# Attention inputs of a decoder: two-part f32r products, a second input buffer, and query and key parts stored once

## The reference, cut to what matters

```
# layer 0, context attention ("ci", then "ca"): queries from x, 1024 keys and values from the context
qh = split_heads(layernorm(x) @ wq.T + bq)
logits = einsum('bhqd,bhkd->bhqk', qh, kh) / sqrt(16)
x = x + (softmax(logits) @ vh) @ wo.T + bo
# layer 1, self-attention ("ai", then "aa"): queries, keys, values from n = layernorm(x), 512 keys
q, k, v = split(n @ qkv_w.T + qkv_b)
x = x + n + softmax(q @ k.T * 0.25) @ v @ fc_w.T + fc_b
```

## Time and profile before

| | us |
|---|---|
| time, median of 3 runs | 5387.59 (5381.12 to 5390.33) |
| profiled execution, its own time | 5385.85 |
| its span | 5384.0 |
| `ci`: first work to the start of `ca` | 913.63 to 984.21 |
| `ca`: first load issued, first scores | 984.21, 1039.29 |
| `ai`: first work to the start of `aa` | 2073.40 to 2193.98 |
| `aa`: first load issued, first scores | 2193.98, 2220.76 |
| mean granted clock of TensorE | 0.956 |

### The profile page before, as it was taken

The page is one execution under the profiler, slowest core; times in us unless marked ns, Lnnn a source line. Parts: engine busy times, 40 slices in busy tenths (PEclk is TensorE's granted clock), DMA queues, the critical chain, the costliest instruction groups (busy, mean ns, idle before and its releaser), DMA issues. The chain is left out here.

```text
span 5384.0 us, 70030 instructions
## 1 busy us (share of the span) xinstructions
PE 4890.0 (91%) x23500; PEld 2615.4 (49%) x23500; DVE 3692.4 (69%) x6760; ACT 2846.1 (53%) x6114; POOL 2464.0 (46%) x1429
## 2 busy tenths in 40 slices
PE   6899996699999798799879999999999999999955
PEld 5555554244444465344455555555555555555423
DVE  8666665588888575577646666666666666666588
ACT  5677772277777433466534444454444445444423
POOL 5555553200000111100037778777777777777700
PEclk9999998699999799799989999999999999999978
DMA  6577676533433004544363433343333333333100
GB/s 213 200 246 253 245 246 207 150 73 69 77 69 73 1 0 162 151 79 80 96 194 83 98 89 85 90 98 82 87 94 83 86 94 93 80 94 94 40 35 20
DMA packets 342964, 593.53 MB, mean 110 GB/s; under 512 B 38576, under 2 KB 131824, under 8 KB 341600
## 3 DMA queue, kind: packets, MB, share of 16 engines
q1 hardware_dynamic: 340448, 585.06, 40.4%
q10 hardware_dynamic: 2176, 4.19, 0.2%
HBM read 333.70 MB, written 221.25 MB: 103 GB/s over the span
## 5 line engine op out<-in xcount | busy, mean ns | idle before, releaser
L2539 POOL TENSOR_TENSOR la_acc<-la_acc,la_pr 128x1024 f32<-128x1024 f32 x704 | 1696.7, 2410 | 494.4 <-ACT la_pr L2497 459.0
L2497 ACT ACTIVATE la_pr<-la_s_ps 128x512 f32<-128x512 f32 x1536 | 793.9, 603 | 971.6 <-PE la_s_ps L2349 970.1
L2356 PE MATMUL la_o_ps<-la_pr,la_vf 128*64 128x512 f32 x3072 | 743.8, 605 | 0.0
L2348 PE MATMUL la_s_ps<-la_q_hl,la_k_hh 128*128 128x512 f32 x1536 | 691.8, 450 | 1.7 <-ACT la_q_hs L2473 1.4
L1757 DVE TENSOR_REDUCE ca_mx<-ca_m_ps 128x2 f32<-128x1024 f32 x512 | 600.7, 1217 | 132.9 <-PE ca_m_ps L1619 132.9
L1720 ACT ACTIVATE ca_pr<-ca_s_ps 128x512 f32<-128x512 f32 x1024 | 541.7, 600 | 255.8 <-PE ca_s_ps L1626 252.6
L2566 DVE TENSOR_REDUCE la_mx<-la_m_ps 128x2 f32<-128x1024 f32 x384 | 463.0, 1206 | 216.8 <-PE la_m_ps L2331 208.8
L2349 PE MATMUL la_s_ps<-la_q_hs,la_k_l 65*128 65x512 f32 x1536 | 608.0, 396 | 0.0
L2566 DVE TENSOR_REDUCE la_mx<-la_misc 128x2 f32<-128x1024 f32 x384 | 466.0, 1214 | 0.0
L113 POOL TENSOR_TENSOR ff_ln_var_eps<-ff_ln_mv,g_eps 128x4 f32<-128x4 f32 x32 | 6.7, 210 | 954.8 <-DVE ff_ln_mv L98 954.8
L2348 PEld LDWEIGHTS la_s_ps<-la_q_hl,la_k_hh 128*128 128x128 f32 x1536 | 290.0, 189 | 242.8 <-ACT la_pr L2497 103.9
(11 more groups left out here) (360 smaller groups left out, 8294.7 us busy)
## 6 DMA issues: line engine op xcount, KB each, us to landing
la_k_hh<-scratch_k_high SPq DMA_DIRECT2D x128, 512.0 KB, 6.5
scratch_k_high<-sc_k_high SPq DMA_DIRECT2D x128, 256.0 KB, 2.6
scratch_k_low<-sc_k_low SPq DMA_DIRECT2D x128, 256.0 KB, 2.8
la_w_parts<-scratch_w_parts SPq DMA_DIRECT2D x64, 512.0 KB, 6.2
la_k_l<-scratch_k_low SPq DMA_DIRECT2D x64, 512.0 KB, 8.4
la_vf<-scratch_xv SPq DMA_DIRECT2D x64, 512.0 KB, 4.1
ca_ks<-scratch_k_rows SPq DMA_DIRECT2D x128, 192.0 KB, 6.3
scratch_vaug<-sc_v SPq DMA_DIRECT2D x16, 1024.0 KB, 4.4
```

The lines of the kernel that those rows point to most:

```text
L2348: pe.matmul(s_ps[:, bank, :], k_hh[:, par, h, keys], q_hl[:, par, h, :], start=True, stop=False)
L2356: last = pe.matmul(o_ps[XD * h:XD * h + XD, :], vf[:, par, st, XD * h:XD * h + XD], pr[:, st % LAG, h, :], start=(st == 0), stop=(st == XT ...
L2497: act.activation(pr[:, st % LAG, h, :], s_ps[:, (2 * st + h) % 3, :], ACT.Exp, scale=scale).then_inc(p_done, 1)
L2539: pool.tensor_tensor(total, total, exps, ALU.add).then_inc(acc_done, 1)
```

## The change

It has four parts.

1. In `ai` the products run on two f32r parts of each operand: high x high, low x high and high x low in place of one f32 product. The weights are split once at the start (ACT copies, POOL subtracts), the turned input per batch (ACT copies `tp` to `x_hi`, DVE subtracts into `x_lo`). In `ci` the product stays f32.
2. The turned input has two buffers (`par`), PE turns batch b+1 ahead of the products of batch b, and normalising runs one batch further ahead. In `ci` POOL's memset of `v1` is gone.
3. `store_parts` writes each part once, four transfers of 256 KB for an operand and batch.
4. `load` repeats the high part: three query and three times `HALVES` key transfers of 16 partitions x 2 heads (64 KB each) stand where one and `HALVES` of 48 partitions stood. A load is 20 transfers in `ca` and 13 in `aa`. The bytes loaded are the same.

The old lines are in the functions above; of the removed ones only those of `store_parts`, the load and the shapes stand here.

```diff
-def store_parts(sp, stack, n, ready, parts, which, stored):
+def store_parts(sp, stack, n, ready, parts, stored):
     for part in range(PARTS):
-        slots = [s for s in range(SLOTS) if which[s] == part]
-        step = slots[1] - slots[0] if len(slots) > 1 else 1
         sp.wait_ge(*ready[part])
         for m in reversed(range(KD)):
-            rows = stack[n, 8 * m:8 * m + 8].rearrange("h (d s) t -> (h d) s t", s=SLOTS)
-            sp.dma_start(rows[:, slots[0]:slots[-1] + 1:step, :],
-                         parts[:, part, m, :].bitcast(F32).unsqueeze(1).broadcast_to([P, len(slots), T])).then_inc(stored, 16)
+            sp.dma_start(stack[n, part, P * m:P * (m + 1), :], parts[:, part, m, :].bitcast(F32)).then_inc(stored, 16)
...
+            w_hi = [pool_.sb(f"w_hi{i}", [P, KD, D], F32R) for i in range(len(names))]
+            w_lo = [pool_.sb(f"w_lo{i}", [P, KD, D], F32R) for i in range(len(names))]
+            x_hi = pool_.sb("x_hi", [P, 2, KD, T], F32R)
+            x_lo = pool_.sb("x_lo", [P, 2, KD, T], F32R)
+        else:
+            xT = pool_.sb("xT", [P, 2, KD, T])
...
+                    if b:
+                        pe.wait_ge(x_high, KD * b)
+                        if own_keys:
+                            pe.wait_ge(x_low, KD * b)
...
+                def project(b, i, ps, ready, low):
+                    par = b % 2
                     for m in range(KD):
+                        cols = slice(m * P, (m + 1) * P)
+                        if b:
+                            pe.wait_ge(low, KD * (b - 1) + m + 1)
+                        for c in range(KD):
+                            if own_keys:
+                                pe.matmul(ps[:, m, :], w_hi[i][:, c, cols], x_hi[:, par, c, :], start=(c == 0), stop=False)
+                                pe.matmul(ps[:, m, :], w_lo[i][:, c, cols], x_hi[:, par, c, :], start=False, stop=False)
+                                last = pe.matmul(ps[:, m, :], w_hi[i][:, c, cols], x_lo[:, par, c, :], start=False, stop=(c == KD - 1))
+                            else:
+                                last = pe.matmul(ps[:, m, :], w[i][:, c, cols], xT[:, par, c, :], start=(c == 0), stop=(c == KD - 1))
+                        last.then_inc(ready, 1)
...
+                turn(0)
+                for b in range(B):
+                    if b + 1 < B:
+                        turn(b + 1)
+                    pe.wait_ge(x_high, KD * (b + 1))
                     if own_keys:
+                        pe.wait_ge(x_low, KD * (b + 1))
+                        if b == 0:
+                            pe.wait_ge(w_low, Q + 1)
+                    elif b == 0:
+                        pe.wait_ge(w_loaded[Q], 16)
+                    project(b, Q, q_ps, q_ready, q_low)
                     if own_keys:
+                        if b == 0:
+                            pe.wait_ge(w_low, V + 1)
+                        project(b, K, k_ps, k_ready, k_low)
+                        values(b)
...
+                    for i in range(len(names)):
+                        act.wait_ge(w_loaded[i], 16)
+                        act.activation(w_hi[i][:, :, :], w[i][:, :, :], ACT.Copy).then_inc(w_high, 1)
...
+                def weight_low(i):
+                    pool.wait_ge(w_high, i + 1)
+                    pool.tensor_tensor(w_lo[i][:, :, :], w[i][:, :, :], w_hi[i][:, :, :].bitcast(F32), ALU.subtract).then_inc(w_low, 1)
+                norm.on_gpsimd(pool, 0, g)
+                if own_keys:
+                    weight_low(Q)
+                norm.on_gpsimd(pool, 1, g)
+                if own_keys:
+                    weight_low(K)
+                    weight_low(V)
+                    pool.memset(v1[:, :, :, :, :], 1.0).then_inc(ones_set, 1)
...
+                def low_x(b):
+                    par = b % 2
+                    for c in range(KD):
+                        dve.wait_ge(x_high, KD * b + c + 1)
+                        dve.tensor_tensor(x_lo[:, par, c, :], tp[:, c, :], x_hi[:, par, c, :].bitcast(F32),
+                                          ALU.subtract).then_inc(x_low, 1)
...
+                moments(0)
+                apply(0)
+                moments(1)
+                if own_keys:
+                    add_x(0)
+                    low_x(0)
+                apply(1)
+                moments(2)
+                for b in range(B):
+                    if own_keys and b + 1 < B:
+                        add_x(b + 1)
+                        low_x(b + 1)
+                    if b + 2 < B:
+                        apply(b + 2)
+                    low_parts(b, q_ps, bq, qparts, q_high, q_low)
+                    if b + 3 < B:
+                        moments(b + 3)
                     if own_keys:
+                        low_parts(b, k_ps, bk, kparts, k_high, k_low)
...
-                        rows = slice(64 * i, 64 * i + STACK)
                         heads = slice(u * GH + i, (u + 1) * GH, 2)
-                        sp.dma_start(qs[rows, u, :, :].bitcast(F32), io[qstack][b, heads].rearrange("h r t -> r h t")).then_inc(loaded[u], 16)
-                        for half in range(HALVES):
-                            sp.dma_start(ks[rows, u, :, half * T:(half + 1) * T].bitcast(F32),
-                                         io[kstack][b * HALVES + half, heads].rearrange("h r t -> r h t")).then_inc(loaded[u], 16)
+                        for s in range(SLOTS):
+                            rows = slice(64 * i + s * DH, 64 * i + (s + 1) * DH)
+                            src = io[qstack][b, QPART[s]].rearrange("(h d) t -> h d t", d=DH)[heads]
+                            sp.dma_start(qs[rows, u, :, :].bitcast(F32), src.rearrange("h d t -> d h t")).then_inc(loaded[u], 16)
+                            for half in range(HALVES):
+                                src = io[kstack][b * HALVES + half, KPART[s]].rearrange("(h d) t -> h d t", d=DH)[heads]
+                                sp.dma_start(ks[rows, u, :, half * T:(half + 1) * T].bitcast(F32),
+                                             src.rearrange("h d t -> d h t")).then_inc(loaded[u], 16)
...
-                        ("q_rows", (B, HEADS, STACK, T)), ("k0_rows", (2 * B, HEADS, STACK, T)), ("k1_rows", (B, HEADS, STACK, T))):
+                        ("q_rows", (B, PARTS, D, T)), ("k0_rows", (2 * B, PARTS, D, T)), ("k1_rows", (B, PARTS, D, T))):
```

169 lines of the change are left out of this document (74 added, 95 removed).

## The result

The changed kernel took 5363.47 us (median of six runs, 5360.86 to 5370.31) where the kernel before took 5383.82 us on the same chip (median of six, 5372.53 to 5390.33). The ratio is 0.9967, its 95% interval 0.9954 to 0.9981: 0.33% faster, beyond the 0.2% that can be told from no change. The forecast of 5383 was 20 us too high; the time lies inside the range of 5358 to 5425, near its lower end. It is rival A's 5362, but only a part of the reason is A's, as the trace shows. The profiled execution of the changed kernel has a span of 5359.4 us and a mean granted clock of 0.955.

A forecast was written before the change was run, and what follows sets the result against it. Bounds taken: TensorE in `ai`, a TensorE-ScalarE ring in `ci`, the DMA queue at the head of `ca`. Terms -22.7 - 7 + 14 + 9 + 2 = -4.7 us gave about 5383 us from 5387.59; range 5358 to 5425.

The forecast's parts named there:

- rival A: Loads of `ca` and `aa`: small loads are cheap, 0.45 to 0.5 us each by SP's issue; 5362 us, chance 0.33.
- its own signs: Prediction wrong if a 64 KB load's price is outside 0.55 to 0.66 us or `ai`'s head takes over 5 us longer.
- t: Price of one 64 KB load to 16 partitions in `ca` and `aa`: taken as 0.60 us, between 0.45 and 1.23.
- Products of two parts: `ai`: 9.8 us a batch instead of 13.19, copy wait gone, longer head; -22.7 us, between -25 and -17.
- D: Rival: DVE bounds `ai` at 10.8 us a batch through tp's PSUM buffer; +8 us, 5391 us, chance 0.05.
- Two buffers in `ci`: `ci`: TensorE's ring opens, DVE becomes the bound, 6.2 us a batch against 7.0; -7 us, bounds -10 and -3.
- Stores: Input phases and scan: smaller stores on a queue that isn't late in either phase; 0, in the scan -2 to +2.
- Loads: Three 64 KB loads for each 192 KB one: +14 us head of `ca`, +9 head of `aa`, +2 steady `aa`.
- C: Rival: loads become the bound of `aa`, from 0.64 us a load; given 5415 us, chance 0.25.
- The sign that was to tell A from B: Window inside `ca`'s first loads: near 107 GB/s shows the forecast, 150 GB/s shows cheap small loads.
- B: The forecast itself: a 64 KB load costs about 0.57 to 0.66 us; 5383 us, range 5374 to 5398, chance 0.37.
- Sum: Whole kernel: -22.7 - 7 + 14 + 9 + 2 = -4.7 us, so about 5383 us.

The follow-up runs named there:

- inputs_only: The changed kernel's new `attention_inputs` with the stores and 48-partition loads of the kernel before; 5357.87 us against 5381.9 for the kernel before, ratio 0.9948.
- layout_only: The kernel before with only the new stores and 16-partition loads, products as before; 5392.33 us against 5381.9 for the kernel before, ratio 1.0020.
- the two profiles of after: Profiles of the changed kernel and of the same code run once more, unedited; measured 5363.47 and 5361.17 us.
- strided_rows: The changed kernel with each 64 KB load's 16 rows going to every third of the 48 partitions; 5399.42 us against 5381.9 for the kernel before, ratio 1.0032.
- halves_in_turn: The changed kernel with consecutive 16-partition loads alternating between partitions 0 to 47 and 64 to 111; 5358.29 us against 5390.08 for the kernel before, ratio 0.9937.

## Why the prediction was off, step by step

By its own signs the prediction failed in two places, though the time fell into its range: `ai`'s head takes 8.5 us longer, over the 5 that were allowed, and in the head of `aa` t comes out at 0.52, under 0.55. In `ai` the error was made good by others, which is luck.

**Products of two parts, -22.7: right in kind, -24.8.** Errors cancelled. From first to last query products `ai` takes 64.7 us, 3.9 less than seven periods of 9.8, and from there to the next phase 14.6, some 2.5 less than the working had; the head lost 4.3 more. The period is 9.20 to 9.24: 128x512 products on f32r operands follow each other at 0.227 us, not 0.24, and 128x256 at 0.12, the low end of the earlier trace rows. The head was by hand 4.2 us longer and is 8.5 longer: the working gave DVE's two first normalisings the steady 1.38 us, and they took 2.47 and 4.88, because the weights' subtractions and the fill on POOL were not free for DVE; the splitting had been counted as lying "beside it, both engines idle there". 1.1 and 3.5 us of stretching, 4.6 in all, account for the 4.3. D did not come: the period is 9.2 us, not 10.8.

**Two buffers in `ci`, -7: mis-sized, -10.6 and -9.8.** The mechanism is as written (DVE the bound, 1.47 us open), the steady period 5.90 instead of 6.2. The seven periods take 38.9 us where they took 50.7, 11.8 us less and not 5: the old ones were 7.2 us in the mean, the new ones are 5.6, with a first of 5.4 and a last of 3.6. The first products start 3.2 us later (11.14 against 7.98 us after the phase's start), where the prediction had the first batch gain 2. The end is 2.0 us shorter by smaller stores (9.9 us from the last query products to the next phase, 11.9 in inputs_only and before). layout_only alone gives `ci` 4.3 us, so here too the stores were worth something.

**Stores, 0: wrong as a price, though not in the sum.** That the queue "isn't late in either phase" is true of before (share 0.85 in the window from 2100 to 2165, shown above), where a batch takes 13.19 us, and with the old products the smaller stores are worth only 1.7 us of `ai` in layout_only. Four MB a batch at 380 GB/s need 11.0 us, and the products were about to need 9.8. The term had to be asked of the kernel after, not of the kernel before. The -22.7 for `ai` held only because the change also cuts the stores to three MB; beside the new products they are worth 16.4 us, nearly all of it as stores that are still running when the products are done.

**Loads: the largest miss. The price was right for a full queue, and the queue isn't always full.** The heads were put at +14 and +9; the two profiles of after show +10.8 and +9.3, +5.7 and +4.7. By the prediction's own terms t = (29.5 + 10.1) / 72 = 0.55 us and (19.7 + 5.2) / 48 = 0.52 us instead of 0.60. These are means of two prices: 0.55 to 0.61 us where the queue is full of 64 KB loads (107 to 119 GB/s), and SP's 0.47 us where it isn't, in the first slot of `ca`'s head (share 0.58) and in steady `aa` (share 0.53). The working used one t for both. The wait on TensorE was put at 29 and is 24.15. A slot of steady `aa` needs some 8.3 us of its 9.63: +2 was forecast, 0 measured; C, which begins at 0.64, stayed away here and came in strided_rows. (The working also took a load of 192 KB as 192 000 bytes. With 196 608 the old load is 1.25 us, and 0.60 us for 64 KB would be 109 GB/s; this changes no term by more than 1 us.)

By the Trainium skill, "SBUF — State Buffer", section "Door 1: The DMA port swizzle (why `[64,N]` ≈ `[32,N]`)", 16 adjacent partitions give 104 GB/s in a transfer of 1 MiB, an estimated 0.63 us for a load here. The trace comes near it where the queue is full in the order of the change, 107 to 119 GB/s; halves_in_turn, at 138 and 146 GB/s, shows what the rule for one transfer leaves out: which partitions its neighbour in the queue goes to.

A's reason, that SP's issue alone is the price, is wrong for most of both heads (share 1.05 to 1.11 in the windows of 64 KB loads) and right in steady `aa` and in halves_in_turn. The sign that was to tell A from B, 107 or 150 GB/s in a window of the head, gives 107 to 119 in windows with these loads alone, but 160 and 146 in longer ones that value loads share.

**Sum.** -22.7 - 7 + 14 + 9 + 2 = -4.7 was forecast; the two profiles of after average -24.9 - 10.2 + 10.1 + 5.2 + 0 = -19.8, and the medians differ by -20.4. Of the 19.4 us between 5382.9 and 5363.47, 3.8 are the starting point: the kernel before was taken at 5387.59, the median of three runs, and has 5383.82 in six. Two thirds of the rest are the heads and steady `aa` (23 + 2 against 15.3, 9.7 us), the rest `ci` (3.2) and `ai` (2.2).

## What to carry to other kernels

When one stage gets faster, price every stream that runs beside it against the new period: a transfer that was hidden by 13 us of products isn't hidden by 9. Look for its cost at the end of the phase, where what has fallen behind is paid at once, and not only in the period. Before cutting loads into pieces by partitions, look at which pieces follow one another in the queue, and let neighbours go to different halves; price a load in a window that holds nothing else; and look for what stands ahead of the one transfer that somebody waits for, since moving it up gave 15 us here, three quarters of what the whole change gave. What a second engine does "beside" DVE in a head of dependent steps can double those steps.
